# Last stage of a two-layer AdaLN kernel: output projections in a row, second four tiles as one group; low parts of the norm stage on VectorE

## What is computed

```python
mod = (silu(c) @ wmod).reshape(B, 6, 1, -1)      # sa, ca, ga, sb, cb, gb; ga, gb kept away from 0
h = layernorm(x) * (1 + ca) + sa
x = x + ga * attention(h)                          # layer 0: 32 heads of 128, 8 key heads, rope, causal
h = layernorm(x) * (1 + cb) + sb                   # layer 1: 32 heads of 16, only scores > 0.001 count
x = x + gb * second(h)                             # layer 0: product with the signs of a weight matrix
                                                   # layer 1: 8 experts of rank 16; the one with the
                                                   #          largest logit is taken, times its logit
```

## Time and profile before

| | us |
|---|---|
| median of 3 runs | 2102.38 |
| lowest, highest | 2100.31, 2106.76 |
| the profiled execution | 2107.49 |
| its span in the profile | 2105.7 |
| PE busy | 1957.5 (93%) |
| DVE busy | 1458.2 (69%) |
| ACT busy | 1076.5 (51%) |
| POOL busy | 1030.7 (49%) |

### The profile page before, as it was taken

One profiled execution on the slowest core, in us unless ns is written; L12 is line 12 of the kernel. 1 busy time (PEld: TensorE's weight loads), 2 busy tenths in 40 slices (PEclk: granted clock), 3 DMA queues, 4 the chain that ended last, 5 costly groups with the idle time before them and its releaser, 6 DMA issues. The chain is left out here.

```text
span 2105.7 us, 33377 instructions
## 1 busy us (share of the span) xinstructions
PE 1957.5 (93%) x11441; PEld 1591.3 (76%) x11441; DVE 1458.2 (69%) x3672; ACT 1076.5 (51%) x2444; POOL 1030.7 (49%) x801
## 2 busy tenths in 40 slices
PE   4899999999999998898848999999999999988897
PEld 3788888888888876576537888888888888856764
DVE  4667767667767667946766666676677666799276
ACT  3556555555555554534235555555556565544422
POOL 3555555545556443434045555656464555424531
PEclk7999999999999999998979999999999999999899
DMA  5010101010010124356330101010101100141551
GB/s 176 21 31 21 31 21 31 21 31 25 27 51 21 61 87 143 108 135 120 83 114 26 31 8 43 21 31 21 31 21 31 51 21 1 31 145 42 135 112 40
DMA packets 132151, 115.84 MB, mean 55 GB/s; under 512 B 43216, under 2 KB 93456, under 8 KB 131984
## 3 DMA queue, kind: packets, MB, share of 16 engines
q1 hardware_dynamic: 125344, 107.08, 17.4%
q10 hardware_dynamic: 6640, 6.63, 1.0%
HBM read 92.67 MB, written 16.81 MB: 52 GB/s over the span
## 5 line engine op out<-in xcount | busy, mean ns | idle before, releaser
L943 ACT ACTIVATE gqa_prob<-gqa_prob,gqa_nmax 128x256 f32<-128x256 f32 (+3 forms) x512 | 284.2, 556 | 152.7 <-DVE gqa_nmax L1074 144.4
L953 ACT CAST gqa_pth<-gqa_pT 128x384 fp32r<-128x384 f32 (+1 forms) x384 | 185.6, 520 | 175.5 <-PE gqa_pT L764 173.1
L1074 DVE CUSTOM_DVE_ANT_0 gqa_prob<-gqa_pS,consts 128x256 f32<-128x256 f32 (+3 forms) x512 | 222.7, 486 | 60.1 <-PE gqa_pS L726 58.1
L1276 POOL TENSOR_TENSOR x<-x,consts 128x512 f32<-128x512 f32 x80 | 107.7, 1346 | 302.1 <-ACT x L927 302.1
L1276 POOL TENSOR_TENSOR y<-y,consts 128x512 f32<-128x512 f32 x80 | 107.5, 1343 | 292.4 <-ACT y L927 292.3
L1082 DVE TENSOR_TENSOR gqa_ptl<-gqa_pT,gqa_pth 128x384 fp32r<-128x384 f32 (+1 forms) x384 | 217.1, 593 | 18.8 <-ACT gqa_pth L953 18.7
L764 PE MATMUL gqa_pT<-consts,gqa_prob 128*128 128x128 f32 x1280 | 183.2, 274 | 15.5 <-DVE gqa_ptl L1082 13.3
L704 PE MATMUL gqa_pj<-first_hh,wqh 128*128 128x512 f32 x496 | 196.5, 396 | 0.0
L704 PE MATMUL gqa_pj<-first_hh,wql 128*128 128x512 f32 x496 | 194.8, 393 | 0.0
L704 PE MATMUL gqa_pj<-first_hl,wqh 128*128 128x512 f32 x496 | 194.3, 392 | 0.0
L764 PEld LDWEIGHTS gqa_pT<-consts,gqa_prob 128*128 128x128 f32 x1280 | 153.5, 141 | 43.8 <-DVE gqa_prob L1098 15.7
(11 more groups left out here) (385 smaller groups left out, 5417.7 us busy)
## 6 DMA issues: line engine op xcount, KB each, us to landing
shared<-in_wo SPq DMA_DIRECT2D x16, 1024.0 KB, 5.1
shared<-in_wq SPq DMA_DIRECT2D x14, 1024.0 KB, 5.5
shared<-in_wmod SPq DMA_DIRECT2D x10, 1024.0 KB, 5.1
raw_kv<-in_wkv SPq DMA_DIRECT2D x14, 512.0 KB, 6.8
vp<-late_hf SPq DMA_DIRECT2D x64, 64.0 KB, 1.8
kp<-late_hf SPq DMA_DIRECT2D x16, 256.0 KB, 2.9
qp<-late_hf SPq DMA_DIRECT2D x16, 256.0 KB, 2.4
qkv_raw<-vp SPq DMA_DIRECT2D x48, 64.0 KB, 3.0
```

What stands on the lines that cost most here:

```text
L943: ins = nc.scalar.activation(p, p, ACT.Exp, scale=-1.0, bias=nmax[r][:, i:i + 1], accum_out=den[r][:, i:i + 1])
L953: nc.scalar.copy(pth[:, n % 2, c:c + w], pT[k % 2][:, 0:w]).then_inc(pt_hi, 1)
L1074: nc.vector.tensor_tensor_reduce(prob[r][:, P_OFF[i]:P_OFF[i] + w], pS[s][:, c:c + w], held.mask[:, T - w:T], -1.0, LARGEST, ALU.add, ALU.min,
L1276: nc.gpsimd.tensor_tensor(rot[r % 2][:], rot[r % 2][:], held.sinT, ALU.mult).then_inc(sined, 1)
```

## The change

In `stage_first`:

- POOL keeps only the clearing of `silu`. The clearing of `y` (128x4096) goes into `stage_groups`, in front of step 1 (in half 1 behind the stores of the last half), and the first `add` waits for it.
- DVE makes all low parts: four `hl` of batch 0, four of batch 1, six of the weights (before: three of the weights and batch 1; POOL had the other seven). In half 1, DVE also makes `hf` and `hh` of batch 1 from PSUM, and ACT makes `hh` of batch 0.

In `stage_heads_and_finish`:

- `kd[1]` is cleared by two memsets on DVE and two on POOL, 128x1024 each, as their first work. POOL clears `bd[2]` in front of chunk 2.
- All eight projections run with only `turn(0)` to `turn(3)` between them, the groups are tiles 0 to 3 and 4 to 7, and bank users, PE, ACT and DVE follow.
- The gated products use the eight score tiles (`sc`, `prob`), so no `gated(j)` waits for an add. DVE adds tiles 0, 5 and 7 (`finish`), POOL the other five.
- In half 0, the statistics of the next input stand between the first residuals, and `next_sums` and `next_scales` behind `choose(0)`.

```diff
@@ stage_first, gpsimd
-                if half:
-                    pool.wait_ge(held.stored, 16 * NT)
-                nc.gpsimd.memset(y[:], 0.0).then_inc(y_clear, 1)
...
-                for k in range(KT):
-                    pool.wait_ge(act_hi, k + 1)
-                    nc.gpsimd.tensor_tensor(hl[:, k, 0:T], hf[:, k, :], hh[:, k, 0:T].bitcast(F32), ALU.subtract).then_inc(pool_lo, 1)
-                weight_los()
@@ stage_first, vector
+                    dve.wait_ge(turned, HB)
                     for k in range(KT):
-                        dve.wait_ge(scaled, k + 1)
-                        nc.vector.tensor_copy(hh[:, k, 0:T], hf[:, k, :]).then_inc(act_hi, 1)
+                        nc.vector.tensor_scalar(hf[:, KT + k, :], pT[KT + k][:], held.modh[:, 0, 1, k, 1:2], held.modh[:, 0, 0, k, 1:2],
+                                                ALU.mult, ALU.add).then_inc(scaled_late, 1)
+                    for k in range(KT):
+                        dve.wait_ge(scaled_late, k + 1)
+                        nc.vector.tensor_copy(hh[:, k, T:2 * T], hf[:, KT + k, :]).then_inc(late_hi, 1)
...
+                for k in range(KT):
+                    dve.wait_ge(act_hi, k + 1)
+                    nc.vector.tensor_tensor(hl[:, k, 0:T], hf[:, k, :], hh[:, k, 0:T].bitcast(F32), ALU.subtract).then_inc(dve_lo, 1)
+                if half:
+                    late_los()
+                for n, (what, i) in enumerate(FIRST_PARTS):
                     dve.wait_ge(split_hi, n + 1)
                     weights.split_lo(what, i, nc.vector).then_inc(dve_split, 1)
+                if half == 0:
+                    late_los()
@@ stage_groups
+                    if d == 0:
+                        dve.wait_ge(y_clear, 1)
...
                 for n in range(NH):
+                    if n == 1:
+                        if half:
+                            pool.wait_ge(held.stored, 16 * NT * half)
+                        nc.gpsimd.memset(y[:], 0.0).then_inc(y_clear, 1)
@@ stage_heads_and_finish
-        zg = [st.sb(f"zg{i}", [P, D]) for i in range(2)]
+        zg = [t[:].rearrange("p t h -> p (t h)") for t in sc + prob]
...
+        groups = [(0, 1, 2, 3), (4, 5, 6, 7)]
+        DVE_ADDS, POOL_ADDS = (0, 5, 7), (1, 2, 3, 4, 6)
@@ scalar
-                    if c < 2:
-                        for j in (2 * c, 2 * c + 1):
-                            nc.scalar.copy(kd[1][:, j].rearrange("p (s r) g -> p s (r g)", r=4), zeros).then_inc(k_zeroed, 1)
@@ vector
-                    if j >= 2:
-                        dve.wait_ge(added, j - 1)
-                    nc.vector.tensor_tensor(zg[j % 2][:], bank("u", j)[:], gb[:, j // TT], ALU.mult).then_inc(z_gated, 1)
+                    nc.vector.tensor_tensor(zg[j], bank("u", j)[:], gb[:, j // TT], ALU.mult).then_inc(z_gated, 1)
+
+                def finish(j):
+                    dve.wait_ge(z_gated, j + 1)
+                    nc.vector.tensor_tensor(x[:, j, :], x[:, j, :], zg[j], ALU.add).then_inc(own_added, 1)
...
+                for j in range(2):
+                    nc.vector.memset(kd[1][:, j], 0.0).then_inc(k_zeroed[0], 1)
...
+                next_stats_of(nexts[0:3])
+                residual(0)
...
+                normalise(0)
+                for j in range(TT, NT):
                     residual(j)
                 normalise(1)
                 choose(0)
+                next_sums()
+                if nexts:
+                    next_scales()
+                gated(0)
+                finish(0)
                 choose(1)
+                for j in range(1, 6):
                     gated(j)
+                finish(5)
                 gated(6)
                 gated(7)
+                finish(7)
@@ gpsimd
+                for j in range(2, 4):
+                    nc.gpsimd.memset(kd[1][:, j], 0.0).then_inc(k_zeroed[1], 1)
                 for c in range(CHUNKS):
+                    if c == 2:
+                        clear_values()
```

More of the change, by code:

```diff
@@ L463, in _ @@
                         nc.scalar.copy(kept[i][:], pM[i][:]).then_inc(mod_kept, 1)
-                for b in range(HB):
+                for b in range(HB if half == 0 else 1):
                     act.wait_ge(turned, b + 1)
@@ L472, in _ @@
                                              scale=held.modh[:, 0, 1, k, b:b + 1]).then_inc(scaled, 1)
-                    for k in range(KT if half == 0 else 0):
+                    for k in range(KT):
                         act.wait_ge(scaled, b * KT + k + 1)
@@ L1708, in stage_heads_and_finish @@
         next_in, tables_in = st.sem("next_in"), st.sem("tables_in")
-        k_zeroed = st.sem("k_zeroed")
+        k_zeroed = [st.sem(f"k_zeroed{i}") for i in range(2)]
         v_zeroed, ones = st.sem("v_zeroed"), st.sem("ones")
@@ L2153, in _ @@
                                             ALU.subtract).then_inc(shifted, 1)
-                for j in range(NT):
+                for j in POOL_ADDS:
                     pool.wait_ge(z_gated, j + 1)
-                    nc.gpsimd.tensor_tensor(x[:, j, :], x[:, j, :], zg[j % 2][:], ALU.add).then_inc(added, 1)
+                    nc.gpsimd.tensor_tensor(x[:, j, :], x[:, j, :], zg[j], ALU.add).then_inc(added, 1)
 def build(nc, a):
```

127 lines of the change are left out of this document (51 added, 76 removed), and 8 rows, old and new, of the table users.

## The result

The changed kernel takes 2086.16 us (median of 5 runs, 2081.55 to 2090.47). The kernel before, run beside it, takes 2102.38 us (2100.31 to 2108.76). The ratio is 0.9908, 95% interval 0.989 to 0.9926: 16.2 us faster by the medians, where 22.3 were forecast. The time lies in the range and on the forecast side, 6.1 us above the forecast.

A forecast was written before the change was run, and what follows sets the result against it. Seams between PE-full attention stages were taken as the bound, each microsecond there counting in full. 2.1 + 5.2 + 2.9 + 2.1 + 4.5 + 6.4 - 0.9 = 22.3 us gave 2080 against the median; range 2072 to 2092.

The forecast's parts named there:

- Norm stage, half 0: End of this stage: DVE's low parts, no longer slowed by POOL, end at 39.6 against 41.7; 2.1 us less.
- Rival C: Norm stages: DVE's subtractions stay slow even without POOL; 5 us of gain left, 2097.4; chance 0.05.
- Norm stage, half 1: Second norm stage: without POOL's memset, DVE's last low part ends at 1091.2 instead of 1096.47; 5.2 us less.
- PE's last transposes then end near 1078.3: Norm stage of half 1: PE finishes transposing just after ACT's four xn end at 1077.27; DVE's row follows.
- First chunks: Start of the last stage: without ACT's clearing copies, keys are issued earlier; 2.9 us gained in half 0, 2.1 in half 1.
- PE can take unit 2 at 959.8 in place of 963.59: 3.6 us: First chunks: keys all issued by 957.6 instead of 961.8, so PE starts this unit 3.6 us sooner.
- the chunks behind it keep some 3.4: First chunks: of the 3.6 us by which unit 2 starts sooner, the following chunks retain about 3.4.
- Rival B: First chunks: they give nothing back, since SP's issues and later keys bound the rest; takes 5.0 us, 2085; chance 0.10.
- Behind the chunks: Last stage from first projection: reordered projections, groups and adds save 4.5 us in half 1, 6.4 in half 0.
- rival A: Behind the chunks PE's clock falls; last four tiles' products take 3.5 us longer; gain 15.9 us, time 2086.5; chance 0.14.
- Attention stages: The moved memset on POOL catches DVE's normalisation; a loss of 0.45 us in each half.
- Rival D: Attention: the memset in step 1 shifts POOL against DVE in later steps, 2.1 us each; slower, 2124; chance 0.03.

The follow-up runs named there:

- w_norm: The changed kernel with extra, unread PE products around the transposes of the norm stage of half 1; 2081.29 us, ratio 0.9893.
- s_split: The changed kernel with two of the four value loads of each unit issued by ACT instead of SP; 2083.1 us, ratio 0.9892.
- p_norm: The kernel before with only the norm-stage edits and the moved clear of y; 2099.78 us, ratio 0.9971.
- p_chunks: The kernel before with only the edits of the clears in the last stage; 2101.27 us, ratio 0.9977.
- n_memset: The changed kernel with POOL's clear of y moved back from the attention to the start of the norm stages; 2084.51 us, ratio 0.9907.

## Why the prediction was right, and where its sizes were off

**Norm stage, half 0 (2.1 us).** Right. From ACT's first high part to the first attention work it takes 13.8 us in all 3 profiles with the old low parts and 11.9 in all 11 with the new ones: 1.9 us. The rest is the 0.3 us between ACT's last high part and DVE's start on it (38.40 to 38.69), which the sum left out. Rival C falls with the first row above.

**Norm stage, half 1 (5.2 us).** Mechanism right, size too large: 3.8 us (20.1 in the mean of 7, against 23.8 in 3). The step that failed is "PE's last transposes then end near 1078.3". It took PE's time as that of ACT's `xn` alone, that is, at the high clock level. PE came out of the seam between two stages and ran much of them at the low one, in all 11 profiles without a fill (PEclk 0.5 to 0.7 over the 32 transposes), the kernel before among them. `w_norm` gives back 1.4 to 1.7 us with the clock up.

**First chunks (2.9 and 2.1 us).** The clears behave as forecast and nothing is caught in them. What they bring is less in half 0: 51.5 us in the mean of 6 against 53.3 in 3, so 1.8; in half 1 it is 49.8 (9) against 52.4 (3), so 2.5. Together 4.4 of 5.0, but each group scatters by 2.5 to 4 us, so each number is good to little more than 1. The step that is off is unit 2 itself, "PE can take unit 2 at 959.8 in place of 963.59: 3.6 us" (these two numbers give 3.8). SP has issued the keys 3.5 us after the stage's first work in every profile with the new clears, as forecast. But PE starts on them at 5.3 to 7.3 us, where the forecast had 5.7, since the landing takes longer in most (PE waits between nothing and 1.87 us, where the prediction's sign was gone or under 1), and with the old clears its start at 9.5 was 8.7 in three of six halves. In the means unit 2 comes 2.9 and 2.5 us sooner and not 3.6.

Of this the chunks keep 1.8 and 2.5, so "the chunks behind it keep some 3.4" fails in size as well. Rival B's mechanism is real in part. PE's later waits for keys are as long in the means as with the old clears (2.2 us against 2.1 in half 0, 2.7 against 3.2 in half 1), but of the profiles with the new clears and SP's old row, those where PE took unit 2 soonest (by 5.8 us) have 1.6 to 4.5 us of them, and the others 0.2 to 2.8. `s_split` took SP's unbroken row of issues apart, and all of these waits went. Rival B's price (nothing left at all) is not what was measured.

**Behind the chunks (4.5 and 6.4 us).** With the clock up and no late gather the stretches are 58.9 and 57.1 us, the forecast was 58.7 (55.7 to the last add, and the 3.0 us that follow it) and 57.2 (56.3 and the barrier of 0.9). The order, the groups and the adds do what was worked out. In the means it is 4.1 us in half 1 (59.2 in 6 against 63.3 in 3) and 6.1 in half 0 (58.5 in 5 against 64.6 in 3). In the first profile of the changed kernel it was 3.7 and 4.1, for two reasons.

- The last products lost the clock: rival A, given 0.14, and one of the prediction's own signs of being wrong. It comes in 7 of the 16 halves with the new order and no fill around them, and in none of 6 with it. It costs 0.6 to 1.2 us and not 3.2. Rival A had all eight products slow, 3.5 us in all; in fact the first four took 3.37 us and the last four 2.23, since PEclk is back at 1.00 from 2079.2 on, so they are 1.7 us longer (5.4 against 3.7). Of this POOL's row of adds and the stores beside it hide about half (last add at 56.3 against 55.5).
- The first projections of half 0 lost it behind the wait for the gather. This I had not looked for, since the one profile of before shows that wait (2.42 us) with the clock at 1.00. Without a fill it fell in all five other profiles with a pause of 1.89 us or more (the kernel with the old order in `p_norm` and `p_chunks` among them), and in none of three with 1.49 to 1.68. It costs 1.7 us in the changed kernel: the last residual starts 31.2 us after the first projection (1035.16, 1003.96) and not 29.5.

**Attention stages (a loss of 0.45 each).** DVE was caught for 0.63 us. In half 1 the stage is not longer: 774.0 in the mean of 10, 774.4 in 4 with the clear elsewhere. In half 0 it is 795.1 against 793.6, a difference of 1.5 with both groups scattered by 2. `n_memset` and the changed kernel's first profile have the same clock after the start and are 0.5 apart. So the forecast loss is likely there. Part of the rest goes with the clock: over the stage of half 0 PE stood at the low level for 18.5 us in the mean of the ten and 16.8 in the four. If half of that difference counts, it is 0.9 us (an estimate from these two means), and 0.6 are left for the memset. No run tested it. Rival D did not occur.

**The sum.** The means of the stretches give 1.9 + 3.8 + 1.8 + 2.5 + 6.1 + 4.1 - 1.5 + 0.4 = 19.1 us. The runs gave 16.2 in the first comparison (ratio 0.9908) and 21.9 in the last (0.9892). So some 3 us of the 6.1 are oversized terms, the norm stage foremost. Much of the rest is likely the base: the median of 2102.38 that the forecast started from was the lowest of five for this kernel, the others lie between 2104.88 and 2106.37. Rival A's 2086.5 is nearer to the measured 2086.16 than the forecast, but by luck. The low clock that it names was there, at about a third of its price; its own ends (59.2 and 59.9) would take 7.1 us and not its 6.4; and the rest came from terms that it shares with the forecast, and from the base.

## What to carry to other kernels

A stretch between two stages is to be read from several executions before a term is built on it: here the same code took 49.3 to 53.3 us in six profiles. Where a short chain of PE work follows a pause, price it at both clock levels and say what decides. When a wait for a load is shortened, look at the queue that issues it: if its row has no gap, the gain ends at the next load, and a load that becomes early lands in front of someone else's.

## What was not expected of the hardware

- Pauses of 1.13 and 0.67 us before the last products cost the clock in 7 halves and left it at 1.00 in 9, with the same work around them. One profile cannot say whether a pause costs the clock; filling it held the clock in 6 of 6 at the last products, in 2 of 3 at the second norm stage.
- DVE and POOL cleared 128x1024 tiles side by side in 0.91 and 0.93 us each, without touching each other, while a POOL memset of 3.52 us held DVE's `xn`, one SBUF tile and two columns of scalars in, for 3.4 us (5.29 in place of 1.92).
- A DVE add of two SBUF tiles beside POOL's adds took 0.81, 1.16, 1.66 or 0.69 us, depending on where in POOL's 1.26 us it arrived.
